# Batch 0's A stage takes over its second group's maxima and the masks' turn, a pattern comes by transfer, and GpSimd sums four steps instead of two

## What is computed

```python
xn = _layernorm(x, axis=-1)
x = x + _L0_attn_ref(xn, ...) + _L0_ffn_ref(xn, ...)
```

```python
scores = jnp.einsum('bhsd,bhtd->bhst', q, k) * scale
attn = jax.nn.softmax(scores, axis=-1)
o = jnp.einsum('bhst,bhtd->bhsd', attn, v_c)
```

```python
sim = (sim - sim.min()) / (sim.max() - sim.min())
pos = sim > 0.9
```

## Time and profile before

| | |
|---|---|
| median of 3 runs | 3130.5 us (3128.25 to 3132.53) |
| the profiled execution | 3128.41 us, span 3126.6 us |
| PE busy | 2953.8 us, 94% |
| DVE busy | 2249.3 us, 72% |
| ACT busy | 1680.2 us, 54% |
| POOL busy | 1137.1 us, 36% |
| mean granted clock of PE | 0.974 |
| first pass | 0 to 196.3 us |
| A of batch 0, then B of batch 0 | from 196.3 us, from about 350 us |

### The profile page before, as it was taken

How to read it: one execution, slowest core, us unless ns; L and a number is a source line. 1 busy time by engine, 2 the same in 40 slices (tenths; PEclk the granted TensorE clock), 3 DMA queues, 4 the chain that set the end, 5 groups by cost and what they waited for, 6 DMA issues and landing times.

```text
span 3126.6 us, 46317 instructions
## 1 busy us (share of the span) xinstructions
PE 2953.8 (94%) x17410; PEld 1298.3 (42%) x17410; DVE 2249.3 (72%) x4021; ACT 1680.2 (54%) x1947; POOL 1137.1 (36%) x616
## 2 busy tenths in 40 slices
PE   5879999999999999999999999999999999999997
PEld 4634433443344443444334433444434443344433
DVE  5765777767777687767777677766777677776792
ACT  2424555545655556545565456545565455654575
POOL 6646322452225512254224522255122542235201
PEclk9979999999999999999999999999999999999999
DMA  4516125300352024511254003430244102540001
GB/s 146 177 29 117 34 67 115 82 16 30 104 98 62 20 64 103 106 27 32 68 113 84 16 30 104 97 63 20 60 103 107 31 30 57 114 96 16 17 17 36
DMA packets 128489, 211.48 MB, mean 68 GB/s; under 512 B 47561, under 2 KB 76137, under 8 KB 128121
## 3 DMA queue, kind: packets, MB, share of 16 engines
q1 hardware_dynamic: 124160, 201.10, 27.2%
q10 hardware_dynamic: 4104, 7.42, 0.6%
HBM read 136.21 MB, written 71.97 MB: 67 GB/s over the span
## 4 chain that ended last, share of the span: by engine, by line
PE 77%; DVE 12%; DMA 3%; POOL 3%; issue 3%; ACT 1%; ACTq 0%; POOLq 0%; SPq 0%; DVEq 0%
PE O L1201 22%; PE M L1102 13%; PE M L1096 10%; DVE mx L1442 10%; PE S L1186 8%; PE S L1189 6%; PE M L1122 4%; PE M L1215 4%; PE M L1166 2%; PE M L1168 2%; PE M L1134 2%; POOL PTx L733 1%; DMA recb_d<-RC 1%; PE M L1111 1%; PE M L1140 1%
## 5 line engine op out<-in xcount | busy, mean ns | idle before, releaser
L1442 DVE TENSOR_REDUCE mx<-M 128x1 f32<-128x512 f32 x3072 | 1973.0, 684 | 620.8 <-PE M L1102 329.2
L950 ACT ACTIVATE PT<-S 128x1024 f32<-128x1024 f32 x1280 | 1241.9, 1022 | 780.8 <-PE S L1189 497.1
L1102 PE MATMUL M<-KB,QB 50*128 50x512 f32 x2048 | 668.8, 482 | 44.8 <-ACT stg L987 11.6
L1102 PEld LDWEIGHTS M<-KB,QB 50*128 50x128 f32 x2048 | 277.5, 186 | 690.4 <-DVE mx L1442 413.1
L1201 PE MATMUL O<-PT,VB 128*32 128x512 f32 x4096 | 559.4, 618 | 0.7 <-ACT PT L950 0.7
L1096 PE MATMUL M<-KA,QA 98*128 98x512 f32 x1024 | 433.6, 470 | 29.7 <-DVE mx L1442 22.0
L783 POOL TENSOR_TENSOR PT<-PT 128x2048 f32<-128x2048 f32 x64 | 292.0, 4563 | 326.2 <-PE O L1201 233.0
L1189 PE MATMUL S<-QB,KB 52*128 52x512 f32 x2048 | 381.3, 437 | 2.9 <-ACT PT L950 2.6
L950 ACT ACTIVATE PTx<-S 128x1024 f32<-128x1024 f32 x256 | 249.9, 1022 | 244.1 <-PE S L1186 243.6
L783 POOL TENSOR_TENSOR PTx<-PTx 128x2048 f32<-128x2048 f32 x64 | 292.2, 4565 | 211.2 <-PE O L1201 138.6
L1096 PEld LDWEIGHTS M<-KA,QA 98*128 98x128 f32 x1024 | 175.6, 191 | 351.2 <-issue 179.1
(11 more groups left out here) (151 smaller groups left out, 1920.3 us busy)
## 6 DMA issues: line engine op xcount, KB each, us to landing
qk_d<-stg SPq DMA_DIRECT2D x32, 1024.0 KB
KA<-kt_d SPq DMA_DIRECT2D x48, 512.0 KB, 7.4
QB<-qk_d SPq DMA_DIRECT2D x192, 128.0 KB
KB<-qk_d SPq DMA_DIRECT2D x192, 128.0 KB
kt_d<-stg SPq DMA_DIRECT2D x16, 1024.0 KB
RB<-recb_d SPq DMA_DIRECT2D x64, 256.0 KB
PT<-in_x SPq DMA_DIRECT2D x8, 1024.0 KB, 5.6
RB<-rec_d SPq DMA_DIRECT2D x32, 256.0 KB
```

The source lines that it names most:

```text
L950: nc.scalar.activation(probs(kind, of_a)[:, 2 * pair:2 * pair + 2, :], Sg[pair][:, :].rearrange("p (j s) -> p j s", j=2), ACT.Exp, scale=S ...
L1102: done = mm(m[:, :], QB[rows, 2 * q + a, at:at + P], KB[rows, 2 * q + a, keys], start=True, stop=True)
L1442: v.tensor_reduce(mx[:, g % 2, unit, kh:kh + 1], m[:, :], AX.X, ALU.max).then_inc(free, 1)
```

## The change

1. `prep_jobs` places the maxima of A's first group alone, two at each place from the sixteenth on, and its turn (`fa`) at the last place. The second group's 32 maxima leave the first pass.
2. `jobs_a(True)`, the jobs of batch 0's A, gets its own places: a table `FIRST_MAXIMA` of how many maxima each of the 32 steps takes (160 in all, 128 before), later places for the turns of the groups (steps 5, 12, 18, 25), for queries and keys of B, and a job `mask` at step 6. `marks` runs on DVE ahead of step 5. SP's `leave_mask` writes the masks to DRAM.
3. `KA`'s pattern is an input `pick`. SP copies it to DRAM, waits, and loads it into 16 rows of `KA`; ACT's eight transfers and POOL's clearing of `KA` go. SP also writes the zeros that ACT wrote. `KB`'s rows of ones come by two transfers, POOL's two fills go.
4. POOL adds four steps: three additions into one buffer, one after the other (`add` in place of `add_pair`), 24 a batch instead of 16. PE forms the denominators once per four steps, at steps 6, 10, ... 30 of A and step 2 of B: 8 a batch instead of 16. `take_dens` moves from the second step of a group to the fourth.

```diff
-    ma = max_units("a", 0) + max_units("a", 1)
-    out = [[] for _ in range(4 * B + 2)]
+    ma = max_units("a", 0)
+    out = [[] for _ in range(4 * B)]
...
-    for i in range(15):
-        out[17 + i] = ma[2 * i:2 * i + 2]
-    out[4 * B] = ma[30:32] + [("fa", "a", 0)] + ma[32:42]
-    out[4 * B + 1] = ma[42:]
+    for i in range(16):
+        out[15 + i] += ma[2 * i:2 * i + 2]
+    out[31] += [("fa", "a", 0)]
...
+FIRST_MAXIMA = (7,) * 4 + (5,) * 12 + (4,) * 2 + (6, 4, 4, 6, 4, 4, 6, 4, 4, 4, 6, 4, 4, 4)
...
+        at = (5, 12, 18, 25)[g] if first else g * NC + 1
+        s[at][1].append(("fa", "a", g + 1) if g + 1 < GA else ("fa", "b", 0))
     if first:
+        s[6][1].append(("mask",))
+        for at, name in ((2, "qk0"), (7, "qk1"), (14, "qk2"), (20, "qk3")):
...
         if kind == "a":
-            return (PT if k % 4 < 2 else PTx)[:, k % 2]
+            at = (k + k // 4) % 4
+            return (PT if at < 2 else PTx)[:, at % 2]
...
+        sp.dma_start(pick_d, io["pick"]).then_inc(sel_in, 16)
+        sp.wait_ge(sel_in, 16)
+        sp.dma_start(KA[A_MAX_ROWS:A_ROWS].bitcast(F32), pick_d).then_inc(sel_in, 16)
...
-        fill((KA[96:P].bitcast(F32), 0.0), (QA[96:P, :].bitcast(F32), 1.0))
-        pool.sem_inc(const_ready, 1)
         normalise(1)
...
-        def add_pair(n, i):
-            k = 2 * i + 1
-            wait_apart(pool, pv_done, n * STEPS + k)
-            wait_apart(pool, e_done, n * (2 * STEPS) + (2 * k + 2))
-            to = probs("a", k - 1)
-            nc.gpsimd.tensor_tensor(to, to, probs("a", k), ALU.add).then_inc(summed, 1)
+        def add(n, i):
+            for j in range(1, 4):
+                k = 4 * i + j
+                if j == 1:
+                    wait_apart(pool, pv_done, n * STEPS + k)
+                else:
+                    wait_apart(pool, summed, n * ADDS + (3 * i + j - 1))
+                wait_apart(pool, e_done, n * (2 * STEPS) + (2 * k + 2))
+                to = probs("a", 4 * i)
+                nc.gpsimd.tensor_tensor(to, to, probs("a", k), ALU.add).then_inc(summed, 1)
...
-            for h in range(HA):
-                row = A_MAX_ROWS + 8 * (h // 4) + h % 4
-                act.dma_start(KA[row:row + 5:4, h, :].bitcast(F32), one_row[0:2, :]).then_inc(sel_in, 16)
...
+                i = of_a // 4
+                if of_a % 4 == 3:
+                    act.wait_ge(dn_done, n * QUADS + i)
+                else:
+                    act.wait_ge(pv_done, step - 2)
+                    act.wait_ge(summed, n * ADDS + (3 * (i - 1) + of_a % 4 + 1))
...
-                if k > NC and k % NC == 1:
+                if k > NC and k % NC == 3:
                     take_dens(n, k // NC - 1)
...
-                if k == 1:
+                if k == 3:
                     take_dens(b, GA - 1)
...
-                if k >= 3 and k % 2 == 1:
-                    denominators(n, b, (k - 3) // 2)
+                if k >= 6 and k % 4 == 2:
+                    denominators(n, b, (k - 6) // 4)
...
-                if k == 1:
-                    denominators(b, b, PAIRS - 1)
+                if k == 2:
+                    denominators(b, b, QUADS - 1)
```

More of the change, by code:

```diff
@@ L133, in jobs_a @@
             s[at][1].append(("po", 4 + c))
+    if first:
+        place_first(s)
+        return s
     for g in range(GA):
@@ L657, in a_steps @@
                     recs(b, "b", GB - 1)
-                if not before and g == 1:
-                    store_fill(0, None, "qk3")
-                    load_b(0, 3)
+                if not before and g in (1, 2):
+                    store_fill(0, None, f"qk{g + 1}")
+                    load_b(0, g + 1)
         def b_steps(b, last):
@@ L1103, in job @@
                               start=True, stop=True)
+            elif kind == "mask":
+                pe.wait_ge(mask_ready, 1)
+                for f in range(2):
+                    done = nc.tensor.transpose(m[:, f * P:(f + 1) * P], masks[:, f, :, :].rearrange("p w c -> p (w c)"),
+                                               ident[:, :])
             elif kind == "fa":
@@ L1550, in a_steps @@
             for k in range(STEPS_A):
+                if not before and k == 5:
+                    marks()
                 for j in (j for part in slots[k] for j in part):
```

129 lines of the change are left out of this document (62 added, 67 removed).

## The result

The changed kernel takes **3111.9 us** (median of 5 runs, 3109.3 to 3117.4) against 3130.5 before: the ratio is 0.994, with an interval of 0.993 to 0.996. It is faster, by 19 us, where 65 were forecast; the value lies outside the range of 3040 to 3095. The profiled execution has a span of 3107.5 us (3126.6 before).

The account below looks back on a forecast made before the run. PE, 94% busy, was taken to bound the kernel outside the first pass. Terms: 3128.4 - 38.0 + 5 - 48.2 + 16.8 = 3064.0 us; with the median 2.1 higher, 3066 us, range 3040 to 3095.

Parts of the forecast that it names:

- Batch 0's A, +5: Batch 0's A: added maxima, DVE's pace, POOL's start-up and marks outweigh denominators saved; +5 us, bounds -5 and +18.
- First pass, -38: First pass: 8.6 us won at its start, 30.2 at its end, 0.8 charged; -38.0 us, bounds -29 and -40.
- My bound of 0: Start of the first pass: lowest gain if DVE paces the last batches; 8.6 us was kept, upper bound 9.6.
- The end, 30.2: End of the first pass: scores start at 166.1 us in place of 196.29, a gain of 30.2 us.
- Denominators, -48.2: Batches 1 to 7: 8 fewer denominators each on PE, 56 x 0.86 us; -48.2 us, bounds -58 and -43.
- the lower of my two ends: PE's time for one denominator: 0.77 us, the lower end; 0.86 was taken and 1.04 was the upper end.
- Start of B, +16.8: Start of each B: PE waits 2.1 us for Z's later transfers, 8 batches; +16.8 us, bounds 0 and 40.
- Z is not waited for: Rival, start of B: other transfers land sooner or PE arrives later; 3066 - 17 = 3049 us, chance 0.12.
- POOL's cover, 0: POOL's chained additions in A finish in time for step 12's exponentials, with 1 us to spare; cost 0.
- The rival of POOL as the bound: A's chained additions cost more than 4.84 us each: 3082 us mildly (0.10), up to 3207 past break-even (0.05).
- Marks, 5: Batch 0's A: DVE's four marks operations wait for POOL's additions; 5 us, bounds 0 and 18.3.
- the signs named beforehand: Right: first scores about 158 us, L1215 about 67 us, additions 4.6. Wrong: ACT or PE idling for L822, scores after 165.

Follow-up runs that it names:

- e8: e7 with sixteen second-group maxima behind the first turn, then five maxima in each of batch 0's A's first sixteen steps and four in the others; 3077.0 us.
- e11: e8 with the first group's maxima from place 18 of the first pass and the marks at step 1; 3067.4 us, ratio 0.982.
- e10: The change with batch 0's A's 160 maxima laid out as six, then five, then four a step, and other turn steps; 3114.1 us, ratio 0.996.
- e1: The change with POOL adding pairs of exponentials again and PE summing 16 times in each A; 3132.8 us, ratio 1.002.
- e9: The change with the first group's maxima beginning at place 18 of the first pass, three each at places 18 to 23; 3111.4 us, ratio 0.994.
- e5: The change with nine of the second group's maxima back behind the first turn, ending the first pass; 3112.4 us, ratio 0.995.
- e13: e11 with POOL adding pairs again and PE summing 16 times in each A; 3125.3 us, ratio 1.000.
- e4: The change with the second group's 32 maxima back in the first pass and four maxima in each step of batch 0's A; 3121.2 us, ratio 0.997.
- e7: The change with nine maxima behind the first turn, Z's transfers first, marks at step 0, B's second row load behind denominators and shift; 3078.6 us, ratio 0.984.
- e12: e6 with marks at step 1, Z's transfers first, B's second row store and load behind denominators and shift; 3082.5 us, ratio 0.984.
- e6: e4 with the marks at step 0 of batch 0's A in place of step 5; 3113.9 us, ratio 0.996.

## Why the prediction was wrong

The sign and the mechanisms of parts were right; the sum missed by 45 us. By the terms, against the profiled execution:

- **Batch 0's A, +5: the step that failed, 20 of the 45 us.** Three sizes in it were wrong. "32 maxima at about a third of a microsecond, 10.6": no row of the forecast showed that price, and the 64 of this kind before took 31.7 us, 0.50 each; the row grew by 47.5 - 31.7 = 15.8 us. "Waits of 9.9 us": 18.9, as a step of five to seven maxima on two banks leaves PE to DVE's pace; I compared DVE's total with the span (115 of 154) and charged 3 us for the four steps of seven alone. And the clock was no term at all: 39 us at the lower level in place of 12, worth some 13 us. The three overlap, as part of the 15.8 is the clock's, and together they are the 20. e8 and e11 show that fewer maxima in A remove it (160.1 and 159.2 us with sixteen of the moved ones back in the first pass), e10 that an even row does not, and e1 that the additions had no part in it. All of that is read from single profiles; of the medians none isolates this term, since what A lost the first pass got.
- **First pass, -38: 31.4.** The start won its 8.2 us by the tenth turn, and lost 7 to a transfer that the forecast did not look at, because it read where the maxima's end moved to and not what their new beginning waits for. My bound of 0, "if the last batches are paced by DVE", was the better end of this term: e9 removed the transfer's wait, and of the 9 us won by it 2.5 at most reached the first scores. The end, 30.2, was about right for its length (the shift at 161.63 stood at 162.7 in the forecast), and A started at half speed behind the bare shift of 6.96 us; e5, with nine maxima in that pause, did so too, so the pause alone is not its cause.
- **Denominators, -48.2: 40 in batches 1 to 7.** 5.7 a batch in place of 6.9. e13 gives 6.2 to a batch of eight sums, 0.78 each, the lower of my two ends. The rest of the gap is that with pairs the changed kernel's A takes 136.6 us (e1), 0.5 more than before; which part of the change costs that was not looked for.
- **Start of B, +16.8: right** in size and place, 2.0 us a batch and a wait of 14.6 us for `Z` in all. What it cost beyond was the clock: 22 us in these stretches between the kernels with the wait and those without. The rival "Z is not waited for" is out.
- **POOL's cover, 0: right.** Additions take 4.56 us, chained ones stand 0.27 apart, and in batch 1's A PE waits for neither POOL nor ACT. The rival of POOL as the bound did not occur.
- **Marks, 5: right in kind, open in size.** In the change PE waited 2.52 us behind them, and the clock was low for the 10.2 us that followed; in e4, e5 and e9 it waited 6.98, 5.92 and 7.90 us, as the marks fell differently against the additions. The rule that I weighed, of the Trainium skill (SBUF — State Buffer, "Who interferes with whom"), agrees with e4 and e9, where a tensor-scalar took 4.58 and 4.49 us and ended with an addition. In e5 it was an operation with two inputs in SBUF, 3.89 us, a kind that the forecast did not count; and of the tensor-scalars on 128x64 there are five, not four.
- **The rest of B, 0: +6.5** in one profile each. The clock falls there now and then in every kernel, for 79 us in all before and 97 after, which at half speed is worth up to 9; how much of it is the change's, these runs do not tell.

Of the signs named beforehand, L1239 with 512 rows and 67.3 us, the gaps of additions, the wait for `Z` and the long operation of marks came as said; the first scores at 164.75 us did not, and stand just short of the 165 that was to show the forecast wrong.

What stays open: why e7 and e8 with 15 us between their A's have medians 1.6 us apart, and how the clock's episodes in B are set off.

## What to carry to other kernels

When work is moved beside other work, do not compare the consumer's total with the span, but count how many pieces a step holds against the buffers between producer and consumer, and leave a free share; where that share went, eight pieces of 0.5 us cost 13, and laying them out more evenly did not bring it back. For work that is moved earlier, look at what its first piece waits for, and when a queue's entry moves behind another, put the one that is needed first in front. A wait of PE is dearer than its length where the granted clock falls behind it (here 22 us for 14.6 us of waits), so short repeated waits come first on the list of what to remove.

## What was unexpected of the hardware

- The `Z` waits sum to 14.6 us, and the stretches that hold them are 22 us shorter without them: short waits of 1.5 to 2.4 us went with time at the lower clock level in 21 of 49 stretches, against 2 of 35 without them.
- An operation of DVE on one element per partition with two inputs in SBUF took 3.89 us beside POOL's addition (e5), like the larger ones on 128x64 (4.58, 4.49); on other occasions the same operations took 0.15 to 0.36.
- A small transfer (denominators to DRAM) that is issued behind loads of B's rows took 6.4 (e10), 6.9 (e12) and 8.6 us (e6) from its issue to that of the next, against 1.8 alone.
- The first addition of POOL in batch 0 stands behind 13 to 18 us of idle time that the profile puts down to nothing (17.69 in the change, 14.40 before, 13.38 in e4_maxima_back). Within that time the trace has two MODIFY_POOL_CONFIG of POOL's queue, at 175.7 us in the change, and the addition starts 7.5 us behind them at 183.16; in every kernel here it is 6.6 to 7.6 us.
